# Last layer: registers and first word loaded within the last norm, and a first step without attention entered by a test of its own

## The reference, cut to what matters

```python
def step(h, p):
    op = jnp.argmax(h[0, 0, :NOPS])
    ...
    y = jnp.einsum('bqk,bkd->bqd', attn, v) @ p['wo'][op]
    h = jnp.where(p['am'][op], y, h)
    z = jax.nn.relu(h @ p['w1'][op] + p['b1'][op]) @ p['w2'][op] + p['b2'][op]
    h = jnp.where(p['fm'][op], z, h)
    return (h, None)
...
fm[0, :] = True
t = t + _L1_ffn_ref(_ln_t(t), ...)
```

## Time and profile before

| | us |
|---|---|
| median of 3 runs (lowest, highest) | 754.9 (753.45, 755.87) |
| profiled execution | 750.22 |
| its span, first to last instruction | 748.4 |
| last layer's first hidden product on PE to the span's end | 585.24 to 748.4 |

### The profile page before, as it was taken

How to read it: one execution, slowest core, us unless ns; L and a number is a source line. 1 busy time by engine, 2 the same in 40 slices (tenths; PEclk the granted TensorE clock), 3 DMA queues, 4 the chain that set the end, 5 groups by cost and what they waited for, 6 DMA issues and landing times.

```text
span 748.4 us, 10687 instructions
## 1 busy us (share of the span) xinstructions
PE 606.9 (81%) x3591; PEld 253.4 (34%) x3591; DVE 571.0 (76%) x589; ACT 440.4 (59%) x662; POOL 471.2 (63%) x250
## 2 busy tenths in 40 slices
PE   4866786887886777876968888988888778999996
PEld 2311121221221222211212223345755235776761
DVE  4498998998998999999999999255564345666644
ACT  3987577578578578577676654444545225555541
POOL 7379999999999999999999999510002110000002
PEclk9998798899998998997898999999999899999999
DMA  4499676566666575666665763000000000000001
GB/s 98 99 291 317 203 251 236 194 256 236 222 229 229 209 262 199 250 244 217 233 236 198 254 229 133 1 1 1 1 12 1 4 19 1 2 1 1 2 1 60
DMA packets 33120, 105.43 MB, mean 141 GB/s; under 512 B 6934, under 2 KB 7455, under 8 KB 33055
## 3 DMA queue, kind: packets, MB, share of 16 engines
q1 hardware_dynamic: 31958, 103.94, 40.8%
q10 hardware_dynamic: 776, 0.55, 0.3%
q0 software_dynamic: 320, 0.13, 0.1%
HBM read 98.84 MB, written 2.10 MB: 135 GB/s over the span
## 4 chain that ended last, share of the span: by engine, by line
PE 43%; DVE 16%; issue 15%; POOL 14%; ACT 8%; DMA 2%; DVEq 0%; SPq 0%; POOLq 0%; ACTq 0%
DVE hh_all L1451 7%; POOL dbu L1761 7%; PE py L716 6%; PE py L229 6%; POOL hc L1750 6%; PE pb L198 6%; PE px L252 5%; DVE pb L1446 4%; PE pb L928 2%; PE pb L704 2%; PE px L743 1%; DMA cc<-scr 1%; PE px L681 1%; PE py L952 1%; PE px L242 1%
## 5 line engine op out<-in xcount | busy, mean ns | idle before, releaser
L1750 POOL TENSOR_TENSOR hc<-hh_all,cc 128x1024 f32<-128x1024 f32 x128 | 299.5, 2376 | 2.3 <-DVE hh_all L1451 1.3
L716 PE MATMUL py<-hc,w_cst 64*64 64x512 f32 x1024 | 156.5, 671 | 25.8 <-POOL hc L1750 17.5
L1451 DVE TENSOR_TENSOR_SCAN hh_all<-da,pb 128x1024 f32<-128x1024 f32 x72 | 164.6, 2286 | 2.5
L1764 POOL TENSOR_TENSOR yg<-w_xs 128x512 f32<-128x512 f32 x10 | 12.6, 1266 | 239.8 <-DVE w_xs L1586 150.2
L1451 DVE TENSOR_TENSOR_SCAN hh_all<-pb,dbu 128x1024 f32<-128x1024 f32 x56 | 127.6, 2279 | 17.1 <-POOL dbu L1761 13.7
L1761 POOL TENSOR_TENSOR dbu<-bb,dtu_all 128x1024 f32<-128x1024 f32 x56 | 133.1, 2377 | 0.0
L704 PE MATMUL pb<-bc,w_sel 128*128 128x512 bf16 x144 | 48.8, 424 | 64.6 <-DVE hh_all L1451 62.0
L1172 ACT ACTIVATE pb<-dt_all,w_aneg 128x1024 f32<-128x1024 f32 x56 | 62.6, 1117 | 58.6 <-DVE hh_all L1451 57.1
L1446 DVE TENSOR_TENSOR pb<-pb,dtu_all 128x1024 f32<-128x1024 f32 x72 | 87.5, 1215 | 1.8 <-DVE dtu_all L1432 0.2
L286 DVE TENSOR_REDUCE gate_all<-pb 128x1 f32<-128x1024 f32 (+7 forms) x64 | 60.4, 985 | 29.4 <-PE pb L198 14.7
L1172 ACT ACTIVATE da<-dt_all,w_aneg 128x1024 f32<-128x1024 f32 x72 | 80.5, 1137 | 0.5
(11 more groups left out here) (291 smaller groups left out, 947.5 us busy)
## 6 DMA issues: line engine op xcount, KB each, us to landing
cc<-scr SPq DMA_DIRECT2D x128, 512.0 KB, 4.3
bb<-scr SPq DMA_DIRECT2D x56, 512.0 KB, 4.8
w_xs<-hc SPq DMA_DIRECT2D x6, 256.0 KB, 4.6
w_xst<-in_x SPq DMA_DIRECT2D x2, 512.0 KB, 5.8
scr<-bcf SPq DMA_DIRECT2D x8, 128.0 KB, 4.3
w_xs<-dt_all SPq DMA_DIRECT2D x4, 256.0 KB, 6.7
w_xs<-dtu_all SPq DMA_DIRECT2D x4, 256.0 KB, 6.4
out<-yg SPq DMA_DIRECT2D x4, 256.0 KB, 3.1
```

The source lines that it names most:

```text
L716: last = nc.tensor.matmul(py[part(t), half(r)], ident[part(r), part(r)], hc[u % NHC][part(r), half(t)], start=(n == 0), stop=(n == NS - 1) ...
L1451: nc.vector.tensor_tensor_scan(hh[u % NHH][:, :], decay[:, :], drive[:, :], 0.0, ALU.mult, ALU.add).then_inc(scan_done, 1)
L1750: nc.gpsimd.tensor_tensor(hc[u % NHC][:, :], hh[u % NHH][:, :], cc[u % NCC][:, :], ALU.mult).then_inc(hc_done, 1)
```

## The change

The control is cut in two: `ready` sets the counters and loads the first word, and `run` takes the registers. PE calls `ready` between `pe_last_dev(pe, 3)` and `pe_last_var(pe, 3)`, ACT between `act_last_sq(act, 3)` and `act_last_rs(act, 3)`, DVE between `dve_h(dve, 2)` and `dve_h(dve, 3)`; POOL and SP call it where `run` did it. In `run` a first test asks whether the word has the feed-forward part and no attention; its body is a `feed`, the next word, and one full step inside a test for the end. Behind this `more` stands in a test for the end of its own; before, its loops were entered without a test.

```diff
-        RUNS, PEELED = (4, 3, 3), 2
+        RUNS = (4, 3, 3)
-        def run(eng, attend, feed, select=None):
+        def ready(eng):
...
             eng.wait_ge(word_done, 1)
             eng.reg_load(word_regs, word[0:1, 0:4]).then_inc(word_read, 1)
+            return word_regs, n_steps, n_att, n_ffn
+
+        def run(eng, state, attend, feed, select=None):
...
-            def peeled(left):
-                if left == 0:
-                    more()
-                    return
+            with eng.If(eng.snap(word_regs[2]) > eng.snap(word_regs[1])):
+                b, e = place()
+                feed(eng, eng.snap(n_ffn), eng.snap(n_att), e, eng.snap(n_steps), b)
+                eng.reg_add(n_ffn, n_ffn, 1)
+                next_word()
                 with eng.If(eng.snap(word_regs[0]) < NSTEP):
-                    step(lambda: peeled(left - 1))
-
-            peeled(PEELED)
+                    step()
+            with eng.If(eng.snap(word_regs[0]) < NSTEP):
+                more()
             return n_steps
...
             pe_last_dev(pe, 3)
+            state = ready(pe)
             pe_last_var(pe, 3)
             pe.wait_ge(h_att, 3)
-            run(pe, pe_attend, pe_feed, pe_select)
+            run(pe, state, pe_attend, pe_feed, pe_select)
...
             act_last_sq(act, 3)
+            state = ready(act)
             act_last_rs(act, 3)
-            run(act, act_attend, act_feed)
+            run(act, state, act_attend, act_feed)
...
-            for c in (2, 3):
-                dve_h(dve, c)
-            run(dve, dve_attend, dve_feed, dve_select)
+            dve_h(dve, 2)
+            state = ready(dve)
+            dve_h(dve, 3)
+            run(dve, state, dve_attend, dve_feed, dve_select)
...
-            run(pool, pool_attend, pool_feed, pool_last)
+            run(pool, ready(pool), pool_attend, pool_feed, pool_last)
...
-            steps = run(sp, sp_attend, sp_feed)
+            steps = run(sp, ready(sp), sp_attend, sp_feed)
```

More of the change, by code:

```diff
@@ L597, in run, with place, next_word, step @@
             eng.reg_load(word_regs, word[0:1, 0:4]).then_inc(word_read, 1)
-            def step(then):
+            return word_regs, n_steps, n_att, n_ffn
+        def run(eng, state, attend, feed, select=None):
+            word_regs, n_steps, n_att, n_ffn = state
+            def place():
                 b = eng.snap(word_regs[0], min_val=0, max_val=NSTEP - 1)
-                e = b * NOPS + eng.snap(word_regs[3], min_val=0, max_val=NOPS - 1)
+                return b, b * NOPS + eng.snap(word_regs[3], min_val=0, max_val=NOPS - 1)
+            def next_word():
+                settle(eng, word_done, eng.snap(n_steps) + 2, passed)
+                eng.reg_add(n_steps, n_steps, 1)
+                eng.reg_load(word_regs, word[0:1, 0:4]).then_inc(word_read, 1)
+            def step():
+                b, e = place()
                 with eng.If(eng.snap(word_regs[1]) > 0):
@@ L622, in more @@
                                     with eng.If(eng.snap(word_regs[0]) < NSTEP):
-                                        step(lambda: None)
-            def peeled(left):
-                if left == 0:
-                    more()
-                    return
+                                        step()
+            with eng.If(eng.snap(word_regs[2]) > eng.snap(word_regs[1])):
+                b, e = place()
+                feed(eng, eng.snap(n_ffn), eng.snap(n_att), e, eng.snap(n_steps), b)
+                eng.reg_add(n_ffn, n_ffn, 1)
+                next_word()
                 with eng.If(eng.snap(word_regs[0]) < NSTEP):
-                    step(lambda: peeled(left - 1))
-            peeled(PEELED)
+                    step()
+            with eng.If(eng.snap(word_regs[0]) < NSTEP):
+                more()
             return n_steps
```

## The result

The changed kernel takes 743.52 us (median of 6 runs, 741.12 to 744.87), the kernel before, beside it, 754.17 (6 runs, 750.14 to 758.34): a ratio of 0.9873, 95% interval 0.9847 to 0.9899. The medians are 10.65 us apart (a quotient of 0.986, within that interval); 8.9 were forecast.

The account below looks back on a forecast made before the run. Bound at the last layer's entry by far branches over untaken bodies, which idle PE and halve its clock, and by empty end loops: 4.7 + 1.8 + 2.4 = 8.9 us, giving 746.0 us, range 743.3 to 749.4.

Parts of the forecast that it names:

- The early load hidden: Last norm: loading the first word early fits in each engine's wait; cost 0, at most 0.8 us without that cover.
- the PE start near 580.4: Last layer's entry: PE can start the first hidden product near 580.4 us, behind its last variance product, instead of 585.24.
- The first test, 4.7 us: Last layer's entry: engines fall into the feed without the far branch over attention, winning 4.7 us.
- the 0.15 allowed: First feed: ACT's first ReLU comes 0.15 us late and sets the pace, as if PE started at 580.5.
- The clock, 1.8 us: First feed: PE stays busy, so TensorE's clock does not fall to half rate; 1.8 us less.
- the clock falls anyway: Rival at the entry: the grant still falls to half, the 1.8 us stay, total 747.8 us; chance 0.12.
- Between the steps, 0: Between first feed and second step: the wait for weights, tests and word handling change nothing; 0 us.
- The gap moves along with the feed: Between the steps: PE's 2.93 us wait for the second step's weights shifts with the feed, winning nothing.
- The end, 2.4 us: Kernel's end: one test replaces four loop rounds, one far branch stays; VectorE drains at 745.8 instead of 748.2.
- the two bounds that were named: Last store's landing at the end: unchanged wins 2.1 us; shortest, 2.6 instead of 3.5 us, puts SP ahead of VectorE.
- The code was on hand: Against the rival that the feed's body must be fetched at entry, PE paying 3.9 us; total 751.6, chance 0.08.
- the far branches did not pay for code that is needed later: Against the slower rival: without far branches, later entries each wait 3.9 us on PE for a fetch; 760.4, chance 0.03.

Follow-up runs that it names:

- e2: Changed kernel with the word loaded in its old place and no test before the end loops, so the first test alone; 750.95 us, ratio 0.9936.
- e7: Changed kernel with the word loaded late again, first test and end test kept; 742.43 us, ratio 0.9875.
- e10: Kernel before with five unread matrix products more on PE, queued ahead of its control at the last layer's entry; 752.73 us, one run.
- e5: Changed kernel with five unread products on PE behind the first feed, while it waits for the second step's weights; 743.56 us, ratio 0.9889.
- e9: Changed kernel with two unread products on PE behind the first feed, while it waits for the second step's weights; 739.75 us, ratio 0.9835.
- e12: Changed kernel without the test before the end loops, third profile of the same program; 744.01 us, one run.
- e1: Kernel before with the early load of the word alone; 751.97 us against 752.48, ratio 0.999.
- e3: Kernel before with the test in front of the end loops alone; 752.69 us against 752.48, ratio 0.9984.
- e4: Kernel before with eleven unread matrix products more on PE, queued ahead of its control at the last layer's entry; 755.45 us, ratio 1.0059.
- e8: The changed kernel as it is, run again beside other variants; 743.71 us, ratio 0.9884.
- e6: Changed kernel without the test in front of the end loops; 746.53 us, ratio 0.9943.
- e11: Changed kernel without the test before the end loops, second profile of the same program; 745.85 us, one run.

## Why the prediction was right, step by step

**The early load hidden: right.** Cost 0. Given the test it wins 0.6 us (e2, e7), not counted in the forecast as a term of its own, since the PE start near 580.4 assumed it.

**The first test, 4.7 us: right, 4.97 measured** with the early load, 4.36 without it (e2). On the time scale of before (less 2.68 us) PE starts at 580.27, ahead of the forecast 580.4, as the hidden product begins at 582.95 while the second pass of the variance product ends at 583.03. ACT is late as forecast: its ReLU at 584.32 follows directly on its last exponential (583.78 + 0.63 = 584.41) and stands 1.37 us behind PE, 0.14 more than the 1.23 of the second step. That it sets the pace does not show: the feed takes 16.19 us against 16.16, so 0.03 of the 0.15 allowed was paid. One reading was wrong without harm: an engine does work in the 2.78 us of the old gap. POOL adds the fourth chunk to the residual there, from 582.53 on, in 1.26 us; the chain of waits does not pass through it.

**The clock, 1.8 us: right, 1.79 measured,** and isolated by e10 (1.80). The rival "the clock falls anyway" is out: in all nine profiles with the first test the feed takes 16.18 to 16.21 us. The half clock in the second step goes when the gap is filled: e5 and e9 are the only two of the 14 profiles without a stretch at half clock in the middle. But the gap alone does not fix where it falls or how long it lasts: it began 18.1 us after the fourth chunk in the changed kernel's profile and 39.1 in e12, where PE came out of the same gap at 2.4 GHz, and it lasted 6.8 us instead of 3.4 in e10. The Trainium skill, TensorE: Matmul & The Clock Gate, Part 1, says that the gate's monitor runs free of the kernel's start; these three agree with it.

**Between the steps, 0: the step that failed.** 0.83 us were won. "The gap moves along with the feed" holds for SP's first issue of weights, which moves by 6.73 us, as the feed's end does by 6.76; but the projection moves by 7.56. SP's timelines show why. The third and fourth weight issue, of the kernel before:

```profile
602.39 2.02 SPq L1880 DMA_DIRECT2D hc<-in_wk  x2
```
```profile
L1880 SPq DMA_DIRECT2D hc<-in_wk x2: 526/774/1023, 602.4 to 603.4; - x2
```

and of the changed one:

```profile
598.31 1.19 SPq L1894 DMA_DIRECT2D hc<-in_wk  x2
```
```profile
L1894 SPq DMA_DIRECT2D hc<-in_wk x2: 545/546/547, 598.3 to 599.0; - x2
```

They take 2.02 us before and 1.19 after, 0.83 less, and that is the whole gain. It has two parts. The pause between the two issues is 0.48 us before and 0.09 after; the other kernels without the first test have 0.47 to 0.48 too (e1, e3, e4, e10), none with the test has it, and what fills it is open. And the fourth issue takes 1.02 us, now 0.55. In e1, e3 and e4 the two issues take 1.96, 2.11 and 1.49, and "to weights" is 2.94, 3.10 and 2.34. In e10 they take 1.49 as well, but "to weights" is 2.74: there the fourth transfer lands 1.73 us behind its issue, in all others 1.34 to 1.53.

The slow fourth issue goes with PE's code. The queues of the kernel before have, from 602.8 to 604.5, besides the weights

```profile
q8 instruction: 1, 0.02, 4.5%
```

a block of 16 KB, in transit from 602.81 to 604.02. The queue is PE's: in e2 it still fetches at 748.5 and 751.5 us, when all other engines have drained. The issue starts while the block is in transit and ends 0.40 us behind it, and so it does in e1 and e3, by 0.40 each. In e4 the block starts 3.8 us ahead of the issue, which takes 0.49 us; in the changed kernel none comes in that stretch. The last store of the output shows the same. In the eight profiles in which it is issued while such a block is in transit (before, changed, e1, e3, e7, e8, e9, e10) it takes 1.07 to 1.75 us and ends 0.23 to 0.37 behind the block, in the other six 0.33. One case fits less well: in e10 the fourth weight issue lies within a block and takes 0.49, and the fifth takes 0.80. So the two go together; by what path a block of PE's code holds up SP is not shown. The Trainium skill, Runtime: NRT & Kernel Launch, Instruction fetch mechanics, says that a sequencer drives its own queue to fetch the next block while it executes, at a cost that is mostly hidden. Whatever the fetch costs PE, SP's rows show it beside SP's slow issues.

**The end, 2.4 us: right, 2.58 measured,** 2.70 alone (e3), 3.0 in the new layout (e6, e11, e12). VectorE and SyncE drain 0.2 us apart, as forecast within a microsecond, SyncE last. The reason given for the stores, that the last two go quicker with the queue to themselves, holds in part. By line:

```profile
L1916 SPq DMA_DIRECT2D out<-yg x4: 333/361/1147, 733.8 to 737.5; - x4
...
DMA to landing us min/median/max: 2.4/2.6/3.1
```

The slowest landing is 3.1 us instead of 3.5, a part of the way between the two bounds that were named; but the last issue still takes 1.15 us. It starts while a block of PE's code is in transit, from 737.26 to 738.25, within PE's far branch, and ends 0.37 us behind it. In e6, where the block starts 0.45 us after the last issue has ended, the four issues take:

```profile
L1915 SPq DMA_DIRECT2D out<-yg x4: 332/344/368, 733.4 to 735.3; - x4
```

**The rivals.** The code was on hand: PE goes from the first test (582.0) to the hidden product (582.95) with no branch or gap of 3 us, and no later entry of the second step has one either, since the middle is not longer in any kernel with the test. So the far branches did not pay for code that is needed later. The one sign of that kind is at the very end, in e2.

The profiled last layer is 10.16 us shorter, 6.76 + 0.83 + 2.58; of the 1.3 us above the forecast, 0.8 are the weights' issues, 0.3 PE's start, 0.2 the end. All three came out on the same side, none makes up for another. The rest between this and the medians' 10.65 is within the spread of the runs: beside e8 the medians are 752.67 - 743.71 = 8.96 us apart, with the same kernels, so whole runs do not test the terms this finely. Counted from the start on the scale of before, the second step's projection stands at 598.53 and the last chunk at 733.53, about 1 us ahead of the 599.5 and 734.6 that were named, by the first two of these terms.

## What to carry to other kernels

Look for a sequencer's branch record, or for a gap between a short branch record and the next instruction, where the chain shows "issue" and no engine on it works: a test that is skipped over a long body cost PE 3.4 to 3.9 us here, the same test fallen through 0.1. Put the likely body directly behind its test, and price with the branch what its silence does to TensorE's clock (1.8 us here). Where PE waits for a transfer on the way, a few unread products that fit in the gap can hold the clock, but count their length by the trace first: two won 1.4 us in the profile, five won nothing.

## What the runs showed that was not expected

- One far branch has no fixed price: on PE over `attend` 3.93, 3.67, 3.37, 3.60 and 3.47 us (before, e1, e3, e4, e10), at the end 3.52 (changed), 3.57 (before) and 4.19 (e6), and in one run 4.41 and 7.58 in a row.
- SP's issue of one 16 KB transfer takes 0.5 us. Issued while a block of PE's code was in transit it took 0.96 to 1.12 in three profiles and 0.49 in a fourth, where the next one took 0.80; the last store took 1.07 to 1.75 instead of 0.33. Some 0.48 of the middle's 0.83 us hang on it.
- Parts that win 0.95 and 6.1 us alone (1.2 with the shorter branch of e1) won 6.8 together: the load and the branch were in the same wait.
- The half clock behind the gap of 2.1 to 3.1 us came in one stretch of 3.4 us in most profiles, and some 20 us later in one, with the same work; in e10 it lasted 6.8 us.
